# Six drains of GpSimd among the experts' row scatters of an AdaLN block

## What is computed

```python
h = layernorm(x) * (1 + ca) + sa
x = x + ga * linear_attention(h)          # 16 heads, causal, then a layer norm
h = layernorm(x) * (1 + cb) + sb
x = x + gb * ffn(h)

def ffn(x):
    x = x + softmax_attention(layernorm(x))       # 16 heads, 8 x 512 tokens
    xf = layernorm(x)
    one_hot = jax.nn.one_hot(jnp.argmax(xf @ gate_w + gate_b), 8)
    y = gelu(xf @ w1[e]) @ w2[e]                  # 8 experts, 128 -> 512 -> 128
    return x + (one_hot * y).sum(experts)
```

## Time and profile before

| | |
|---|---|
| runs | 711.34, 712.17, 712.18 us; median 712.17 |
| the profiled execution | 712.04 us, its span 709.9 us |
| busy share of the span | PE 89%, DVE 83%, ACT 70%, POOL 60% |
| mean granted clock of PE | 0.963 of full speed |
| transfers issued by POOL | 32 at L755, 39 at L884 |

### The profile page before, as it was taken

How to read it: one execution, slowest core, us unless ns; L and a number is a source line. 1 busy time by engine, 2 the same in 40 slices (tenths; PEclk the granted TensorE clock), 3 DMA queues, 4 the chain that set the end, 5 groups by cost and what they waited for, 6 DMA issues and landing times.

```text
span 709.9 us, 16403 instructions
## 1 busy us (share of the span) xinstructions
PE 632.1 (89%) x5448; PEld 330.1 (46%) x5448; DVE 586.2 (83%) x1296; ACT 493.9 (70%) x1007; POOL 424.1 (60%) x965
## 2 busy tenths in 40 slices
PE   4599789989977898999999999999999998977994
PEld 2367556666655222223333333322323323877994
DVE  5877998998867988899999999999999964645552
ACT  3634666676554378888889888888888888524662
POOL 6212657667555754346676777878878736543553
PEclk9899999999999689999999999999999999978998
DMA  6564134235253221146200303012030003615500
GB/s 181 178 211 127 60 91 141 102 117 179 90 181 112 68 90 46 45 124 206 68 24 12 102 24 112 13 46 85 19 113 13 24 35 95 188 69 154 146 31 12
DMA packets 42898, 66.25 MB, mean 93 GB/s; under 512 B 7948, under 2 KB 36335, under 8 KB 39808
## 3 DMA queue, kind: packets, MB, share of 16 engines
q1 hardware_dynamic: 39232, 56.73, 26.3%
q0 software_dynamic: 3296, 8.41, 3.3%
q10 hardware_dynamic: 288, 0.07, 0.0%
HBM read 41.64 MB, written 22.26 MB: 90 GB/s over the span
## 4 chain that ended last, share of the span: by engine, by line
PE 62%; ACT 16%; DVE 10%; issue 6%; POOL 3%; SPq 1%; another core or an unknown queue 1%; DMA 1%; POOLq 0%; DVEq 0%; ACTq 0%
PE bank L1087 14%; PE pair L1076 9%; ACT arena L1999 8%; PE bank L1048 7%; PE pair L1337 5%; PE bank L1098 3%; DVE arena L1572 3%; PE pair L1346 2%; PE bank L1346 2%; PE bank L942 2%; ACT arena L1968 2%; DVE arena L1408 2%; PE bank L931 2%; POOL arena L654 2%; PE pair L1128 2%
## 5 line engine op out<-in xcount | busy, mean ns | idle before, releaser
L1999 ACT ACTIVATE arena<-pair 128x512 f32<-128x512 f32 x506 | 277.9, 602 | 49.1 <-PE pair L1076 46.3
L1572 DVE TENSOR_REDUCE arena<-bank 128x1 f32<-128x512 f32 x388 | 251.8, 684 | 7.8 <-PE bank L1048 6.4
L1076 PE MATMUL pair<-q_stack,k_stack 64*128 64x512 bf16 x506 | 158.2, 386 | 6.4 <-ACT arena L1999 5.1
L1048 PE MATMUL bank<-k_stack,q_stack 63*128 63x512 bf16 x388 | 136.8, 395 | 7.0 <-DVE arena L1572 4.1
L1087 PE MATMUL bank<-arena,values 128*9 128x512 f32 x1024 | 133.9, 595 | 1.6 <-ACT arena L1999 1.5
L1408 DVE TENSOR_TENSOR arena<-bank,cst 128x512 f32<-128x512 f32 x128 | 82.0, 682 | 24.6 <-PE bank L916 24.1
L1572 DVE TENSOR_REDUCE arena<-pair 128x1 f32<-128x512 f32 x124 | 84.5, 682 | 1.8 <-PE pair L1048 1.4
L719 POOL TENSOR_TENSOR arena<-arena 128x32 f32<-128x32 f32 (+6 forms) x312 | 68.8, 220 | 24.4
L1048 PEld LDWEIGHTS bank<-k_stack,q_stack 63*128 63x128 bf16 x388 | 33.1, 93 | 106.6 <-ACT arena L2004 25.8
L1076 PEld LDWEIGHTS pair<-q_stack,k_stack 64*128 64x128 bf16 x506 | 40.6, 93 | 49.2 <-ACT arena L1999 24.3
L2135 ACT ACTIVATE fq_all<-pair 128x512 f32<-128x512 f32 x39 | 23.3, 596 | 40.9 <-PE pair L1337 27.7
(11 more groups left out here) (298 smaller groups left out, 1249.1 us busy)
## 6 DMA issues: line engine op xcount, KB each, us to landing
softmax_parts<-arena SPq DMA_DIRECT2D x8, 768.0 KB, 4.1
q_stack<-softmax_parts SPq DMA_DIRECT2D x48, 128.0 KB
k_stack<-softmax_parts SPq DMA_DIRECT2D x48, 128.0 KB
linear_parts<-arena SPq DMA_DIRECT2D x7, 768.0 KB, 3.7
q_stack<-linear_parts SPq DMA_DIRECT2D x42, 128.0 KB
k_stack<-linear_parts SPq DMA_DIRECT2D x42, 128.0 KB
arena<-in_L_ffn_w_dram SPq DMA_DIRECT2D x16, 256.0 KB, 4.5
v_all<-token_rows SPq DMA_DIRECT2D x20, 192.5 KB, 2.5
```

Of the source, the lines that this page charges most:

```text
L1048: pe.matmul(bank[:], qs[b % 2][rows, slot, qt * P:(qt + 1) * P], ks[b % 2][rows, slot, :], start=True, stop=True).then_inc(d_s_m, 1)
L1076: pe.matmul(score_bank(s)[:], ks[u][rows, 2 * g + x, kt * P:(kt + 1) * P], qs[u][rows, 2 * g + x, :], start=True, stop=True).then_inc(d_s_ ...
L1572: dve.reduce_max(mx[:, m % 2, col:col + 1], bank[:], AX).then_inc(d_s_mr, 1)
L1999: act.activation(pt[:, kt % 2, x, half, :], score_bank(s)[:], ACT.Exp, scale=SCALE).then_inc(d_s_e, 1)
```

## The change

POOL's loop over the last 35 tiles gets a drain behind every fourth scatter, for j = 11, 15, 19, 23, 27 and 31. A drain lets the engine go on only when its pipeline is empty. It carries no semaphore. Nothing else is changed; the order of the other instructions is the same on every engine. Lines behind L901 are two higher in the new file.

```diff
                 for j in range(4, MT):
                     scatter_out(j)
+                    if j % 4 == 3 and 8 < j < MT - 4:
+                        pool.drain()
                 pool.wait_ge(s_sc, 16 * MT)
```

## The result

The change made the kernel **slower**: 716.75 us (714.77 to 717.48, five runs) against 712.17 (711.34 to 712.76, five runs), a ratio of 1.0066 with a 95% interval of 1.0052 to 1.0079. The forecast was 707.0 us.

What follows compares the result with a forecast made beforehand. PE was taken to carry the kernel (89% busy, 62% of the chain), with POOL's closing drain holding its end. 712.04 + 0 on the path - 5.2 off the tail = 706.8, forecast 707.0 us; 8-in-10 range 706.0 to 709.6.

Steps and rivals of the forecast that it cites:

- What a drain costs: On POOL: 0.081 us for each transfer issued since its last drain, about 5.8 us over 71 transfers.
- the tail: End of the span, 703.30 to 709.90: 6.60 us with no engine busy and no byte moving, laid to POOL's closing drain.
- The 5.2 us off the tail: At the program's end: closing drain finds 7 scatters instead of 71 transfers, 64 x 0.081 = 5.2 us saved, bounds 4.7 to 5.9.
- That a drain waits for the landing and makes POOL late: POOL behind scatters 11 to 31: landing 2.4 us quiet, 3.4 loaded; scatter 12 starts 3.5 us late, scatter 32 2.3.
- Cost on the path: nothing: End of POOL's loop: scatter 32's 2.3 us lateness is made up, scatter 38 starts at 701.49 as before; cost 0.
- slack of 2.86 us: POOL, scatters 32 to 38: six intervals of 1.28 make 7.7 us where 10.54 were taken.
- Rival 1: POOL still late at the end, landings 2.9 to 3.4 us all along: 1.0 to 3.4 us given back, 708.0 to 710.4; chance 0.18.
- Rival 2: At the program's end: a drain does nothing that the tail waits for; time stays 712.2 us; chance 0.10.
- Rival 3: POOL behind scatters 11 to 31: drain's price fixed, 734 us, or through all transfers since the start, 726; chance 0.10.

Runs made afterwards that it cites:

- the third chip: The change itself, six drains of POOL, against the kernel before on another chip, where that takes 697.43 us: 693.62 us, ratio 0.9951.

## Why the prediction was wrong, point by point

- **What a drain costs: right.** The forecast had 0.081 us a transfer, taken from the length of the tail over 71; measured 0.082. That it met the figure so closely is in part luck, as it took the middle of 5.5 to 6.6 us. The 5.2 us off the tail came to 5.26.
- **That a drain waits for the landing and makes POOL late: right, and near in size.** Gaps of 2.4 to 2.5 us quiet for 2.3, 3.3 loaded for 3.3; the first 5.8 for 4.4. The forecast let the whole price of the older transfers pass while scatter 11 was under way. The trace has its landing 4.0 us after its start (3.4 were taken) and the drain's end 1.86 us behind that, so half of the price came on top.
- **"Cost on the path: nothing": this step failed.** It counted the lateness of POOL against a slack of 2.86 us and took PE, DVE and ACT as untouched "to 0.1 us", since nobody waits for a scatter. The catching up behind each drain, three or four scatters 1.28 us apart, held up DVE's and ACT's starts by 1.3 to 3.5 us, and PE's last product came 10.6 us late, over half of it in one stall and the stretch at the lower clock behind it.
- **Rival 1** (POOL still late at the end) is what the third chip shows: 3.8 us faster. **Rival 2** is refuted by the tail. **Rival 3** named the right side, slower, with a wrong mechanism: the price is not fixed, and the tail did shorten. Its chance of 0.10 stood for the only road to slower that I had thought of.
- The evidence was in the trace of the kernel before: two groups of close scatters, and in each a wait for "remote" of 2.5 and 5.0 us while every local producer was done. I took the back-to-back rows as proof that 1.28 us is a harmless rate, and did not look at what the other engines did beside them.

## What to carry to other kernels

A closing drain of GpSimd costs 0.08 us for each transfer that it issued since its last one, so a kernel with many of them can take part of that off its end with a drain, but only at a place where GpSimd waits anyway. Before pausing an engine "off the critical path", ask at what rate it will work off the backlog. Then look in the trace of before at stretches where it already works at that rate: what the *other* engines do there is the answer. Where a wait ends in "remote" in a program of one core, compare the times at which the semaphores changed with the ends of the rows that change them. Such a wait is worth an experiment before it is worth a theory, and a second chip is worth more than more runs on one.

## What the runs showed of the hardware

- GpSimd's closing drain, behind transfers that have all landed, takes 0.082 us for each one issued since its last drain (5.876 us behind 71, 0.618 behind 7). A drain in the midst of the work waits for the newest to land and ends 0.04 us for each behind that (0.20 us behind 4, 1.86 behind 44).
- Indirect DMAs of GpSimd 1.28 us apart, three or more in a row, go with late signals of PE on some chips: DVE and ACT start 1.1 to 10.3 us late, the more the longer the group. Several signals then arrive within 0.2 to 0.3 us. At 1.8 us apart none was late, at 1.5 us some in long rows; of pairs none but one, with a third scatter 1.61 us behind it.
- It was there in the runs of the result (kernel before 712.2 us) and on the first, fourth and fifth chips (712.5 to 713.8 us), and not on two (696.9 and 697.4 us), for the same programs. **Open:** what differs between the chips, and what holds the signals up.
